# Attention phase of a two-layer kernel: the router's input on ScalarE and GpSimd, q's first half on VectorE, another common order of the steps

## The reference, cut to what matters

```python
mod = silu(c) @ wmod                    # per sequence: shift, scale, gate for a and b
h   = layernorm(x) * (1 + scale_a) + shift_a
q   = rope(h @ Wq + bq); k = rope(h @ Wk + bk); v = h @ Wv + bv
att = softmax(where(causal, -inf, q @ k.T / sqrt(16)))
x1  = x + gate_a * ((att @ v) @ Wo + bo)
h2  = layernorm(x1) * (1 + scale_b) + shift_b    # the router's input
logits = h2 @ Wg + bg
```

## Time and profile before

| what | value |
|---|---|
| median of 3 runs | 1154.22 us (1152.57 to 1155.61) |
| profiled execution | 1155.28 us, its span 1153.5 us |
| attention phase | 0 to about 456 us of the span |
| TensorE, VectorE | busy 1011.4 us (88%), 724.4 us (63%) |
| ScalarE, GpSimd | busy 610.8 us (53%), 474.5 us (41%) |
| mean granted TensorE clock | 0.948 |

### The profile page before, as it was taken

One profiled execution on the slowest core, in us unless ns is written; L12 is line 12 of the kernel. 1 busy time (PEld: TensorE's weight loads), 2 busy tenths in 40 slices (PEclk: granted clock), 3 DMA queues, 4 the chain that ended last, 5 costly groups with the idle time before them and its releaser, 6 DMA issues. The chain is left out here.

```text
span 1153.5 us, 19010 instructions
## 1 busy us (share of the span) xinstructions
PE 1011.4 (88%) x6150; PEld 561.1 (49%) x6150; DVE 724.4 (63%) x1540; ACT 610.8 (53%) x1149; POOL 474.5 (41%) x703
## 2 busy tenths in 40 slices
PE   4679899999999995599998855999999998999996
PEld 3234444444444442356564532656666665444543
DVE  1758888888888863633342223767678873466856
ACT  2358678687777774023332224434444443887862
POOL 2554546445564410268888873334233410000000
PEclk9689999999999998599999987999999998999997
DMA  5622305234252303456766771021211002002001
GB/s 165 115 48 30 84 25 107 68 72 99 38 107 49 58 30 84 149 135 136 164 140 163 173 117 29 6 66 42 79 43 38 19 20 92 1 9 64 28 28 55
DMA packets 74443, 85.81 MB, mean 74 GB/s; under 512 B 12602, under 2 KB 68674, under 8 KB 74218
## 3 DMA queue, kind: packets, MB, share of 16 engines
q1 hardware_dynamic: 61994, 67.79, 23.0%
q0 software_dynamic: 12288, 16.79, 8.5%
q10 hardware_dynamic: 64, 0.02, 0.0%
HBM read 45.26 MB, written 25.21 MB: 61 GB/s over the span
## 5 line engine op out<-in xcount | busy, mean ns | idle before, releaser
L644 DVE TENSOR_REDUCE nmax<-psum 128x1 f32<-128x512 f32 (+3 forms) x352 | 210.3, 635 | 31.6 <-PE psum L879 29.2
L766 ACT ACTIVATE pT<-psum 128x512 f32<-128x512 f32 x320 | 178.9, 596 | 39.8 <-PE psum L909 19.1
L879 PE MATMUL psum<-k6T,q6T 122*128 122x512 bf16 (+3 forms) x512 | 126.3, 314 | 21.8 <-DVE nmax L644 19.5
L1190 POOL DMA_INDIRECT residual<-expert_y,idx_e x64 | 101.2, 1582 | 25.2 <-issue 17.4
L1709 DVE TENSOR_TENSOR l_scores<-psum,const_sb 128x512 f32<-128x512 f32 x128 | 79.4, 683 | 19.4 <-PE psum L1884 19.3
L879 PEld LDWEIGHTS psum<-k6T,q6T 122*128 122x128 bf16 x512 | 43.5, 99 | 93.0 <-DVE nmax L644 69.1
L920 PE MATMUL psum<-pT,v 128*32 128x512 f32 x640 | 85.0, 604 | 0.0
L1177 POOL DMA_INDIRECT expert_tokens<-router_input,idx_e x64 | 63.5, 992 | 50.0 <-POOLq L1010 30.8
L904 PE MATMUL psum<-q6T,k6T 125*128 125x512 bf16 x192 | 70.7, 382 | 5.1 <-ACT pT L766 4.0
L1842 PE MATMUL psum<-l_hT,l_w 128*128 128x512 f32 x128 | 65.0, 631 | 1.6 <-ACT l_hT L1777 0.9
L2345 PE MATMUL psum<-c_x0T,c_w 128*128 128x512 f32 x128 | 61.7, 615 | 0.4
(11 more groups left out here) (297 smaller groups left out, 2264.5 us busy)
## 6 DMA issues: line engine op xcount, KB each, us to landing
q6T<-q_parts SPq DMA_DIRECT2D x96, 128.0 KB, 4.4
expert_w<-in_ew SPq DMA_DIRECT2D x16, 768.0 KB
x_in<-in_x SPq DMA_DIRECT2D x8, 512.0 KB, 4.1
residual<-x SPq DMA_DIRECT2D x32, 128.0 KB, 1.9
router_input<-h SPq DMA_DIRECT2D x32, 128.0 KB, 1.8
l_x<-residual SPq DMA_DIRECT2D x8, 512.0 KB, 7.2
x_dram<-l_x SPq DMA_DIRECT2D x32, 128.0 KB, 1.7
out<-c_out SPq DMA_DIRECT2D x16, 256.0 KB, 2.1
```

The costliest lines, as they stand in the source:

```text
L644: dve.tensor_reduce(nmax[:, i, u * nh:(u + 1) * nh], ps_s[:, n % SR, 0:nh * (i + 1) * P].rearrange("p (h k) -> p h k", h=nh), AX_X, ALU.ma ...
L766: act.activation(pT[:, n % PR].rearrange("p h t -> p (h t)"), ps_t[:, n % TR, :], ACT.Exp, scale=HD ** -0.5).then_inc(probs, 1)
L879: last = pe.matmul(out[:, a], q6T[0:MASK_ROWS, b % 2, u * nh + a, i * P:(i + 1) * P], keys[:, first:first + step_by * i + 1:step_by, :], s ...
L1190: pool.indirect_dma_start(out=rows, out_offset=bass.IndirectOffsetOnAxis(ap=m.idx_e[:, e, i:i + 1], axis=0), in_=y[:, e % YS, i, :], in_of ...
```

## The change

Four edits.

1. The router's input. VectorE's two steps per tile go. GpSimd adds two small steps behind `rstd2` that give `nbias2`, ScalarE normalises x1 to `xn2` (two buffers), and GpSimd multiplies by the scale row and adds the shift row, each a step of 128x256 with two operands in SBUF.
2. The start. VectorE, no longer GpSimd, casts the mask rows and the identity, and for the first half of the first sequence also does GpSimd's part of turning and splitting q. GpSimd so comes to the keys first.
3. `rows` is moved from ahead of the first `kT` to just ahead of the first `mT`; its copy out of PSUM goes to ScalarE; VectorE's eight steps for two gates become four over both. The store and the loads go, on SyncE, behind the second `mT`; the gate of sequence 0 behind the third.
4. All places of the common order get new numbers.

```diff
 ATTENTION_PLACE = {
-    "ln": -197,
+    "ln": -200.53,
...
-    "S": [[-58, -31, -19, -16], ...
+    "S": [[-58.78, -17.12, -13.7, -6.8], ...
...
-    order.insert(order.index(("kT", 0)), ("rows", 0))
+    order.insert(order.index(("mT", 0, 0)), ("rows", 0))
     for b in range(B):
-        order.insert(order.index(("sp", b, 1) if b else ("st", 1)) + 1, ("gate", b))
-    for first, later in ((("kv", 0), ("Q", 0, 1)), (("sp", 0, 0), ("kv", 0))):
+        order.insert(order.index(("sp", b, 1) if b else ("mT", 0, 2)) + 1, ("gate", b))
+    for first, later in ((("kv", 0), ("Q", 0, 1)), (("sp", 0, 0), ("Q", 0, 1))):
...
 (sync)
-                        if b == 0 and half == 1:
+                    if s == ("mT", 0, 1):
+                        sp.wait_ge(rows_final, 1)
+                        sp.dma_start(m.mod_rows[:, 0:4 * C], rows[:]).then_inc(rows_stored, 16)
+                        sp.wait_ge(rows_stored, 16)
+                        for first in range(3):
+                            load_rows(first)
...
 (gpsimd)
-                    if s[0] == "Q":
+                    if s[0] == "Q" and s != ("Q", 0, 0):
...
-                    if s[0] == "sp":
+                    if s[0] == "sp" and s != ("sp", 0, 0):
...
                         link(pool.tensor_scalar(vtmp2[:, i:i + 1], mv2[:, i, 1:2], EPS, None, ALU.add))
-                        pool.tensor_tensor(rstd2[:, i:i + 1], vtmp2[:, i:i + 1], mhalf[:, 0:1], ALU.pow).then_inc(rstd2_ready, 1)
+                        link(pool.tensor_tensor(rstd2[:, i:i + 1], vtmp2[:, i:i + 1], mhalf[:, 0:1], ALU.pow))
+                        link(pool.tensor_tensor(vtmp2[:, i:i + 1], mv2[:, i, 0:1], rstd2[:, i:i + 1], ALU.mult))
+                        pool.tensor_scalar(nbias2[:, i:i + 1], vtmp2[:, i:i + 1], -1.0, None, ALU.mult).then_inc(nbias2_ready, 1)
+                    if s[0] == "h2":
...
+                        pool.wait_ge(xn2_ready, t + 1)
+                        settle(pool, m.passed)
+                        pool.tensor_tensor(h2[:, b % 2, i, :], xn2[:, t % 2, :], rowb[:, b % 3, 1, :], ALU.mult).then_inc(h2_scaled, 1)
+                        pool.wait_ge(h2_scaled, t + 1)
+                        settle(pool, m.passed)
+                        pool.tensor_tensor(h2[:, b % 2, i, :], h2[:, b % 2, i, :], rowb[:, b % 3, 2, :], ALU.add).then_inc(h2_ready, 1)
...
 (vector)
+                        if n == 0:
+                            link(dve.tensor_tensor(qb[:], qb[:], rope[:, 1, :], ALU.mult))
+                            dve.wait_ge(y_drain, y_use[s] + 1)
+                            dve.tensor_tensor(qf[:], qa[:], qb[:], ALU.add).then_inc(q_sum, 1)
+                    if s == ("sp", 0, 0):
+                        dve.wait_ge(q_hi, 1)
+                        dve.tensor_tensor(qf[:], qf[:], qs[:, 0, 0, :], ALU.subtract).then_inc(q_rest, 1)
+                        dve.wait_ge(q_mid, 1)
+                        dve.tensor_tensor(qs[:, 0, 2, :], qf[:], qs[:, 0, 1, :], ALU.subtract).then_inc(q_lo, 1)
...
 (scalar)
+                    if s[0] == "rows":
+                        act.wait_ge(row_fill, 1)
+                        act.activation(rows[:], ps_row, ACT.Copy).then_inc(row_copy, 1)
+                    if s[0] == "h2":
+                        _, b, i = s
+                        t = NT * b + i
+                        act.wait_ge(nbias2_ready, t + 1)
+                        if t >= 2:
+                            act.wait_ge(h2_scaled, t - 1)
+                        act.activation(xn2[:, t % 2, :], x1[:, b % 2, i, :], ACT.Identity, bias=nbias2[:, i:i + 1],
+                                       scale=rstd2[:, i:i + 1]).then_inc(xn2_ready, 1)
```

More of the change, by code:

```diff
@@ L388, in step @@
                                          qs[:, half, part, :]).then_inc(q_placed[b % 2][half], 16)
-                        if b == 0 and half == 1:
-                            sp.wait_ge(rows_final, 1)
-                            sp.dma_start(m.mod_rows[:, 0:4 * C], rows[:]).then_inc(rows_stored, 16)
-                            sp.wait_ge(rows_stored, 16)
-                            for first in range(3):
-                                load_rows(first)
                     if s[0] == "mT":
@@ L597, in step @@
                         dve.tensor_copy(cols[:].unsqueeze(2), m.modT[:, 0, 0:4, b:b + 1]).then_inc(cols_ready, 1)
-                    if s[0] == "rows":
-                        dve.wait_ge(const_loaded[0], 16)
-                        dve.wait_ge(const_loaded[1], 16)
-                        dve.tensor_copy(m.ident_bf[:], m.const[:, C_IDENT:C_IDENT + P]).then_inc(ready, 1)
-                        dve.wait_ge(row_fill, 1)
-                        dve.tensor_copy(rows[:], ps_row).then_inc(row_copy, 1)
+                        if b == 0:
+                            dve.wait_ge(mask_loaded, 16)
+                            dve.tensor_copy(phi[K_ROWS:P, :].rearrange("p (i t) -> p i t", i=NT),
+                                            mask[K_ROWS:P, 4:5, :].to_broadcast([P - K_ROWS, NT, P])).then_inc(mask_ready, 1)
+                            for n, at, tiles in ((0, own_tile(0), 3), (0, own_tile(3), 1), (1, plain_tile(0), 3),
+                                                 (2, even_tile(0), 4), (3, odd_tile(0), 4)):
+                                for turn in range(2):
+                                    dve.tensor_copy(k6T[K_ROWS:P, turn, at * P:(at + tiles) * P].rearrange("p (i t) -> p i t", i=tiles),
+                                                    mask[K_ROWS:P, n:n + 1, :].to_broadcast([P - K_ROWS, tiles, P])).then_inc(mask_ready, 1)
+                            dve.wait_ge(const_loaded[0], 16)
+                            dve.wait_ge(const_loaded[1], 16)
+                            dve.tensor_copy(m.ident_bf[:], m.const[:, C_IDENT:C_IDENT + P]).then_inc(ready, 1)
```

110 lines of the change are left out of this document (50 added, 60 removed).

## The result

The changed kernel takes 1166.92 us (median of 4 runs, 1165.21 to 1168.39), the kernel before, beside it on the same chip, 1154.31: a ratio of 1.0103, 95% interval 1.0084 to 1.0123. The forecast was 1140 us, range 1126 to 1155. The sign is wrong, and the time lies in the band of the rival to which 0.12 was given (1161 to 1174), though mostly not for that rival's reason.

The account below looks back on a forecast made before the run. The prediction took TensorE to bound the attention loop (94% busy), with gaps from waits on other engines. Start -8.8, loop -7.5 and end +2.3 summed to -14.0 us on the median of 1154.2: 1140 us, range 1126 to 1155.

Parts of the forecast that it names:

- the rival to which 0.12 was given: Loop: GpSimd becomes what the loop waits for, at the next sequence's keys; 1161 to 1174 us, chance 0.12.
- The start, -8.8 us: First sequence: earlier `xn`, keys and first scores save 8.8 us up to the first transposed scores, bounds -10 and -4.
- Both cost nothing so: Start: SyncE's store and loads behind the second `mT`, and GpSimd's gate behind sequence 1's keys, cost 0 us.
- I take the 11.3 us of waits for `nmax` as gone: Loop: TensorE's waits for VectorE's `nmax`, spread over 22 places, all go: -11.3 us.
- The wait for `k` doubled, +3.8: Loop: TensorE's wait for GpSimd's keys doubles under GpSimd's added steps, +3.8 us over seven sequences.
- The bound of +26: Loop term's upper bound: 3.7 us per sequence, nearly all that is added ahead of the keys, seven times.
- The last rival: Start gives half (half clock under the rows' product, q's transfers late), loop nothing: 1152.5 us, chance 0.06.
- the signs of being wrong: Loop: the period staying at 48.9 us, or TensorE's longest waits naming GpSimd's `k` or `msp`.
- The end, +2.3: End of attention: ScalarE's last-tile step stands ahead of sequence 6's logits, +2.3 us, bounds 0 and +4.
- The slower rival's rule: Loop: if slow work were all that counts, GpSimd's slower steps cost +16 us in place of -7.5, near 1164.
- VectorE loses 5.95 us per sequence: Loop: router's two steps leaving VectorE free it of 5.95 us per sequence, from 15.8 + 8.0 us for 16 tiles.

Follow-up runs that it names:

- e3: The changed kernel with router's input back on VectorE and the old table of places, so the new start alone: 1156.1 us, 1.0008 of the kernel before.
- e1: The changed kernel with all places of the common order as before; start and router's input stay changed: 1174.3 us, 1.0175 of the kernel before.
- g3: f2 with router's input back on VectorE as before the change: 1144.2 us, 0.9904 of the kernel before.
- f2: f1 with the sends of q's parts also placed earlier in SyncE's order: 1152.4 us, 0.9977 of the kernel before.
- e2: The changed kernel with router's input back on VectorE; start and new places stay: 1158.7 us, 1.0030 of the kernel before.
- f1: The changed kernel with heads 12 and 13 of query tile 1 asked for later (place -32.76 to -5.5): 1158.7 us, 1.0029 of the kernel before.
- f4: e1 with the third tile's scaling moved from place 175 to 190, behind the next keys: 1158.5 us, 1.0026 of the kernel before.
- e4: The changed kernel with the sends of q's parts placed earlier in SyncE's order, nothing else moved: 1172.4 us, 1.0155 of the kernel before.

## Why the prediction was wrong, point by point

- **The start, -8.8 us: right, 1.1 too much.** `xn` starts at 10.06 us (forecast 9.8), first scores at 32.70 (32.0), first transposed scores at 60.74 (59.5), -7.7 in all; the keys of sequence 1 come 9.5 us sooner. But e3 shows what the term didn't say: the new start by itself brings the first transposed scores 4.5 us sooner and the keys of sequence 1 0.4, and the rest came with the new places. "Both cost nothing so" holds for the gating only in those: in the old ones it stood ahead of the keys (e3).
- **"I take the 11.3 us of waits for `nmax` as gone": wrong, the term that failed first.** Of 11.3 us 9.0 stayed. The longest wait shrank from 1.2 to 0.6 us. Two pairs of runs price what router's input has to do with these waits, each in one order: 5.1 us in the old one (e3 11.3, e1 6.2), 4.3 in the new one (g3 14.6, f2 10.3). The trace of before said so, for each of the 22 waits, by what VectorE did just ahead of the maximum that ended it. One sequence of it on VectorE, then on TensorE (the second router step, 1.51 us, is in the earlier trace rows):

```profile
260.92 0.75 DVE L635 SCALAR_TENSOR_TENSOR q_product<-psum,bq_sb,rope_sb 128x512 f32<-128x512 f32 x1 [2.10 <-ACT q_swapped L726]
261.59 0.55 DVE L644 TENSOR_REDUCE nmax<-psum 128x1 f32<-128x384 f32 x1
262.06 0.56 DVE L678 SCALAR_TENSOR_TENSOR h<-x,mv,rowb 128x256 f32<-128x256 f32 x1
...
264.09 2.18 DVE L644 TENSOR_REDUCE nmax<-psum 128x1 f32<-128x384 f32 x4
...
262.19 0.34 PE L879 MATMUL psum<-k6T,q6T 122*128 122x384 bf16 x1 [0.66 <-DVE nmax L644]
264.69 0.34 PE L879 MATMUL psum<-k6T,q6T 122*128 122x384 bf16 x1 [0.79 <-DVE nmax L644]
```

  The wait at 264.69 is of the kind that the term counted: router's steps stand ahead of the maximum. There are six of these, 5.1 us. The wait at 262.19 has `q_product` ahead, which stays: six, 4.0 us. Before nine more, 2.0 us, VectorE idled until the scores came, and the wait is the maximum's own time. One more, 0.2 us, has only other maxima ahead. The prediction named router steps and small steps for "the long ones" and took the rest with them.
- **The wait for `k` doubled, +3.8: right to 0.2 us** (3.8 to 7.4), **by luck.** The doubling was a guess, and it is the sum of two things that the prediction didn't part: the new places by themselves take the wait down to 1.6 us (e2, g3), and the move adds 5.8 in them (g3 1.6, f2 7.4). The bound of +26 wasn't out of reach: in the old places, e1 has 15.9 us of these waits and loses 18.2 against e3. The tile that mattered was the third, which the new table sets behind the keys.
- **The transfers of q's parts in the loop: never costed.** The prediction read the new table for GpSimd's tiles ahead of Q, and counted SyncE's queue at the start only. What it put at nothing costs 14.6 us by f1 and f2: 8.2 for heads 12 and 13, asked for first, and 6.4 more for the sends. It is the largest term, and without it the kernel is at 1152.4, 0.9977 (0.9965, 0.9989) of the kernel before beside it. `sp` of half 1, nine places later, is the third number that bears on it; no run moves it alone. The last rival has q's transfers late, but at the start only; none has them in the loop. Nor do the signs of being wrong: of TensorE's longest waits they name `k` and `msp`, and the longest was for q's parts.
- **The end, +2.3: sized 0.6 too low.** The mechanism held: sequence 6's logits behind the last `xn`, 2.70 us of wait. The move's price at the end is 2.9 us by g3 and f2. Of the rest of the 5.0, 1.9 went with q's waits between after and f2 (81.3 and 79.4). What the 2.9 holds besides the wait is the clock, below.
- **The slower rival's rule**, 32 tiles x 2 x (0.73 - 0.48) = +16 us, which stood beside the Trainium skill's GPSIMD Engine Reference, Engine selection, gives none of the measured prices: the move costs 8.2 us in both new orders, and 18.2 in the old one, where the place of one tile's steps decides over 15.8 (f4). The direction the page gives holds in all three.
- **"VectorE loses 5.95 us per sequence": 5.4 measured, but 2 of the 5.95 belong to the places, not to the move.** The second router step on VectorE over all 32 tiles, in before and then in g3 (min/median/max ns):

```profile
L681 DVE SCALAR_TENSOR_TENSOR h<-h,rstd,rowb x32: 484/485/1518, 111.7 to 450.2; 128x256 f32<-128x256 f32 x32
L688 DVE SCALAR_TENSOR_TENSOR h<-h,rstd,rowb x32: 483/485/609, 105.5 to 441.0; 128x256 f32<-128x256 f32 x32
```

  In before 12 of the 32 overlap GpSimd's `q_turned` step of two operands (L493) and take 1.47 to 1.52 us; the other 20 take 0.48 to 0.49. In g3 none overlaps it. With the new places the two router steps cost VectorE 8.1 + 7.6 us for 16 tiles (e2 and g3), 3.9 per sequence; in the old ones, 15.8 + 7.9 (e3). After's loop has hardly any VectorE step left that doesn't read a bank, so whether the 64 added GpSimd steps would hold one up can't be seen in it. The rule of shared ports (the Trainium skill, SBUF — State Buffer, section SBUF: two separate sides) fits the twelve: two steps with two SBUF inputs each, and one held until the other ends.

## What to carry to other kernels

When a change brings a new common order, read that order per queue for each transfer: when its data are ready, what stands ahead of its issue, and which consumer asks first; here one score step asked 27 places too early and cost 8.2 us. A wait named after an engine is not the time you get back by unloading that engine: count only the waits in which it was busy with the work that goes. And work moved to an idle engine costs by what it stands ahead of: 1.5 us ahead of the keys cost 15.8 us in all, as idle time and as clock, the same steps behind them nothing of it.

## What the runs showed of the hardware

Waits of TensorE of some 2 to 4 us can cost more than themselves, and need not. In after's end the granted clock and what it does to the last transposes (stretches from 458.60 and 462.00 us), and the same four transposes of g3, where no wait is longer than 0.6 us:

```profile
458.60:462.00 3.40, 0.70 (x17) 0.43 (x18) 0.32 (x2) 1.45 (x3) 2.17 (x7) 1.00 0.00 0
462.00:467.00 5.00, 3.01 (x20) 1.61 (x24) 0.00 (x0) 1.53 (x4) 2.12 (x3) 0.59 0.32 109
```
```profile
439.00:444.80 5.80, 3.04 (x40) 1.62 (x40) 2.33 (x6) 2.01 (x6) 0.86 (x2) 1.00 0.28 93
```

Behind an idle stretch of 2.70 us the clock fell to a mean of 0.59, near the lower of its two levels (1.2 in place of 2.4 GHz), a transposed tile took 1.16 us from copy to copy in place of 0.91, and the last products 1.08 in place of 0.65: some 1.2 us on a wait of 2.7. A wait of that kind isn't needed for it: in before the clock fell at 452.67, with no wait over 0.6 us in the 10 us ahead, and the last products took 0.96.

In the loops the clock fell and came back within some 5 us. In after one wait of 2.96 us did that, and one of 2.10 did not (the wait, then the 5 us from its end and from the end of the other):

```profile
144.20 0.38 PE L906 MATMUL psum<-k6T,q6T 122*128 122x256 bf16 x2 [2.96 <-DMA q6T<-q_parts]
...
144.20:149.20 5.00, 5.00 (x21) 3.53 (x22) 2.50 (x6) 2.55 (x5) 1.53 (x6) 0.66 0.01 3
249.34:254.34 5.00, 5.00 (x47) 3.41 (x51) 3.42 (x9) 3.60 (x8) 2.19 (x7) 1.00 0.02 4
```

TensorE is busy in all of both stretches. In e4 the clock fell at the waits before 145.25, 199.05 and 304.61 (3.01, 2.97 and 3.66 us), not at those before 252.16 and 357.60 (2.70 and 2.56). In e1 it fell at the keys' waits before 184.67, 235.32, 286.21 and 336.87 (1.83, 1.83, 2.11, 1.82 us), not at those before 134.89 and 387.82 (2.04 and 1.83); the mean over 160 us was 0.96. In g3, whose longest wait in the loop is 0.9 us, it stayed at 1.00. So a wait's length alone doesn't tell whether the clock falls; what does was not measured.
